# Sorting the nodes of a graph network by type, so that both typed node stages run one type per batch

## The reference, cut to what matters

```python
def typed_linear(inp_, W, b):                       # W: 3 x 256 x 256
    y = jnp.einsum('ni,tio->tno', inp_, W) + b[:, None, :]
    return y[node_type, ar]

h = relu(layernorm(x));  x = x + L0(h, ...)         # k, q, v of all nodes; edges; x + h + agg @ Wo.T + bo
h = relu(layernorm(x))                              # 6250 x 256
k, q, v = typed_linear(h, Wk, bk), typed_linear(h, Wq, bq), typed_linear(h, Wv, bv)
# per edge: softmax of q[dst] . (k[src] @ rel_att[type]) over the edges of one (dst, relation)
t_rel = segment_sum(w * (v[src] @ rel_msg[type]))   # n x 6 x 256
t = (t_rel * present).sum(1) / max(present.sum(-1), 1)
trans = typed_linear(t, Wa, ba)
alpha = sigmoid(skip)[node_type]
out = trans * alpha + h * (1 - alpha)
normed = layernorm(out) * ln_g[node_type] + ln_b[node_type]
return x + where(has_msg, normed, h)
```

## Time and profile before

| | |
|---|---|
| median of 3 runs | 4629.6 us (4625.82 to 4632.87) |
| the profiled execution | 4623.52 us, its span 4621.4 us |
| TensorE, VectorE busy | 87%, 88% of the span |
| GpSimd, ScalarE busy | 73%, 63% |
| mean granted TensorE clock | 0.929 of full |
| DMA | 945 MB, mean 205 GB/s |

### The profile page before, as it was taken

The page is one execution under the profiler, slowest core; times in us unless marked ns, Lnnn a source line. Parts: engine busy times, 40 slices in busy tenths (PEclk is TensorE's granted clock), DMA queues, the critical chain, the costliest instruction groups (busy, mean ns, idle before and its releaser), DMA issues. The chain is left out here.

```text
span 4621.4 us, 112678 instructions
## 1 busy us (share of the span) xinstructions
PE 4013.6 (87%) x23424; PEld 3321.3 (72%) x23424; DVE 4065.6 (88%) x13278; ACT 2903.7 (63%) x8405; POOL 3360.6 (73%) x3824
## 2 busy tenths in 40 slices
PE   5888888888888879999798989998988898878887
PEld 2477777777777759899577777777767776757777
DVE  6789999999999975555699999999999999978898
ACT  5755555555555533333688888888888888872222
POOL 4588888888888841010688888888888888867776
PEclk9999999999999989999888888888898888888899
DMA  4687777777777766665677777777777777766665
GB/s 157 203 252 230 227 229 227 230 228 228 229 228 229 228 156 194 203 199 185 182 207 205 205 205 205 206 205 205 205 205 205 205 205 205 205 163 196 182 183 140
DMA packets 647340, 945.24 MB, mean 205 GB/s; under 512 B 215284, under 2 KB 490461, under 8 KB 646987
## 3 DMA queue, kind: packets, MB, share of 16 engines
q0 software_dynamic: 153792, 510.82, 39.7%
q1 hardware_dynamic: 493451, 433.34, 32.3%
HBM read 772.80 MB, written 171.02 MB: 204 GB/s over the span
## 5 line engine op out<-in xcount | busy, mean ns | idle before, releaser
L1438 POOL DMA_INDIRECT kv1c<-kv_table,rec x936 | 916.5, 979 | 299.0 <-issue 175.3
L794 POOL DMA_INDIRECT kv<-kv_table,rec x864 | 920.4, 1065 | 246.8 <-issue 231.3
L1492 ACT ACTIVATE wv<-kv1c,wv 128x64 f32<-128x64 f32 x3744 | 927.7, 334 | 2.2
L1570 DVE CUSTOM_DVE_ANT_0 masked_scores<-score_p,mask 126x384 f32<-126x384 f32 x1248 | 679.8, 545 | 6.7 <-issue 3.7
L1668 PE MATMUL sum_p<-wv,hot 128*126 128x260 f32 x1872 | 615.3, 475 | 0.9 <-ACT wv L1492 0.9
L961 PE MATMUL sum_p<-msg,hot 128*126 128x256 f32 x1728 | 432.8, 394 | 190.4 <-DVE msg L917 190.4
L1630 PE MATMUL qe_p<-qrel,hotT 126*128 126x256 f32 x1872 | 547.2, 436 | 20.4 <-ACT hotT L1470 14.0
L1427 POOL TENSOR_SCALAR hot<-iota,local 128x126 f32<-128x126 f32 x936 | 549.1, 599 | 0.2 <-issue 0.2
L961 PEld LDWEIGHTS sum_p<-msg,hot 128*126 128x126 f32 x1728 | 309.0, 189 | 278.2 <-DVE msg L917 211.2
L1630 PEld LDWEIGHTS qe_p<-qrel,hotT 126*128 126x128 f32 x1872 | 427.7, 229 | 106.8 <-ACT hotT L1470 14.2
L1668 PEld LDWEIGHTS sum_p<-wv,hot 128*126 128x126 f32 x1872 | 391.5, 224 | 85.6 <-ACT wv L1492 1.7
(11 more groups left out here) (247 smaller groups left out, 10238.6 us busy)
## 6 DMA issues: line engine op xcount, KB each, us to landing
key<-segment_keys SPq DMA_DIRECT2D x312, 189.0 KB
q_blk<-q_table SPq DMA_DIRECT2D x216, 192.5 KB, 3.5
acc_table<-acc SPq DMA_DIRECT2D x312, 128.0 KB
qrel<-q_by_relation SPq DMA_DIRECT2D x312, 126.0 KB
acc_in<-acc_table SPq DMA_DIRECT2D x50, 767.8 KB
q_by_relation<-qrel SPq DMA_DIRECT2D x50, 756.0 KB
feat<-in_edge_feat_t SPq DMA_DIRECT2D x216, 128.0 KB, 3.6
agg_table<-total SPq DMA_DIRECT2D x216, 126.0 KB
```

The lines of the kernel that those rows point to most:

```text
L794: pool.indirect_dma_start(kv[k][:, t, :], None, c["kv0_d"], bass.IndirectOffsetOnAxis(ap=rec[k][:, t, 0:1].bitcast(I32), axis=0)).then_inc ...
L1438: pool.indirect_dma_start(kv[k][:, t, :], None, c["kv1_d"], bass.IndirectOffsetOnAxis(ap=rec[k][:, t, 0:1].bitcast(I32), axis=0)).then_inc ...
L1492: ins = act.activation(wv[k][:, t, h, 0:DK], kv[s][:, t, D + h * DK:D + (h + 1) * DK], ACT.Copy, scale=wv[k][:, t, h, DK:DK + 1])
L1570: dve.tensor_tensor_reduce(junk[k][:, h, :], score_p[:, h, :], mask[it.slot(4)][:], 1.0, -BIG, ALU.add, ALU.max, top[s][:, h:h + 1]).then_ ...
```

## The change

`prepare` sorts the nodes by type on the chip. From the types (126 x 50) it makes, by masks, a scan and two small products, the place of each node in a list in which each type fills whole batches of P = 128; 52 batches hold all (`BATCHES`). It writes the list as `who_d` (per place: the node's number, once clipped for reading and once beyond the table for an empty place, so that a store skips it), made by 50 products of a one-hot matrix of batches (126 x 52) with one of lanes (126 x 128), and `type_of`, the type of each batch, in SBUF.

`nodes_1` and `nodes_out` go over 52 batches in place of 50 groups. An engine that needs the type loads it into a register (`reg_load`, the row TENSOR_LOAD below) and addresses the resident weights, biases and gains by it. The masks, the masked copies, the sums over three types and the gathers of typed rows are gone. In their place GpSimd gathers the aggregate and `xh` (one table now), scatters k, v and q by relation to the rows of their nodes, gathers the accumulators (1560 numbers a node in one row) and scatters the output. `x1` and `h1` stay in the order of the list in one table.

```diff
@@ prepare
+                pe.wait_ge(in_batch_ready, 2)
+                for j in range(GROUPS):
+                    if j % LANE_STEP == 0:
+                        pe.wait_ge(in_lane_ready, j // LANE_STEP + 1)
+                    ins = pe.matmul(who_p[:], in_batch[:, j, :], in_lane[:, j, :], start=j == 0, stop=j == GROUPS - 1)
+                dve.wait_ge(kinds_loaded, 64)
+                for t in range(TYPES):
+                    link(dve.tensor_scalar(of_type[:, t, :], kind_in[:], float(t), None, ALU.is_equal))
...
+                dve.tensor_tensor(in_batch[:], lanes(lane[0:GROUP, 0:BATCHES], GROUPS), spread(batch_f[:], BATCHES),
+                                  ALU.is_equal).then_inc(in_batch_ready, 1)
+                dve.tensor_tensor(in_batch[:], in_batch[:], spread(node_id[:], BATCHES), ALU.mult).then_inc(in_batch_ready, 1)
+                for j in range(0, GROUPS, LANE_STEP):
+                    some = slice(j, j + LANE_STEP)
+                    dve.tensor_tensor(in_lane[:, some], lanes(lane[0:GROUP, :], LANE_STEP), spread(lane_f[:, some], P),
+                                      ALU.is_equal).then_inc(in_lane_ready, 1)
@@ nodes_1, GpSimd
-                    pool.indirect_dma_start(bias[k][:], None, w0["b_kvq1"],
-                                            bass.IndirectOffsetOnAxis(ap=kind_col[k][:], axis=0)
+                    pool.indirect_dma_start(agg_xh[k][:], None, c["agg_xh_d"][0:NP, :],
+                                            bass.IndirectOffsetOnAxis(ap=who_in[k][:, 0:1], axis=0)
+                    pool.indirect_dma_start(c["kv1_d"], bass.IndirectOffsetOnAxis(ap=who_out[k][:, 1:2], axis=0),
+                                            kv[k][:], None, bounds_check=NP - 1, oob_is_err=False
+                    pool.indirect_dma_start(qrel_rows, bass.IndirectOffsetOnAxis(ap=who_out[it.slot(UN)][:, 1:2], axis=0),
+                                            qrel[k][:], None, bounds_check=NP - 1, oob_is_err=False
-                run_stages(pool, GROUPS, ((1, gather),), UN)
+                run_stages(pool, BATCHES, ((0, gather), (6, scatter_kv), (7, scatter_rel)), UN)
@@ nodes_1, VectorE
-                    dve.tensor_tensor(hT_rest[k][:], hT[k][:], hT_lead[k][:], ALU.subtract).then_inc(hT_split, 1)
+                    dve.tensor_tensor(hT_rest[k][:], hT_p[:], hT_lead[k][:], ALU.subtract).then_inc(hT_split, 1)
-                run_stages(dve, GROUPS, ((6, q_rest), (2, residual), (1, kinds), (3, scale), (4, split_kinds),
-                                         (4, h_rest), (5, kvq_out), (7, rel_out)), UN)
+                run_stages(dve, BATCHES, ((6, q_rest), (2, residual), (3, scale), (4, h_rest), (5, kvq_out),
+                                          (7, rel_out)), UN)
@@ nodes_1, TensorE
+                    pe.reg_load(kind, c["type_of"][0:1, ds(it.index, 1)])
+                    t = pe.snap(kind, min_val=0, max_val=TYPES - 1)
-                        for a in range(KINDS):
+                        for a in range(HALF):
+                            row = ds(t * HALF + a, 1)
-                            pe.matmul(dst, lead, w_lead[:, a, cols], start=a == 0, stop=False)
+                            pe.matmul(dst, lead, w_lead[:, row, cols], start=a == 0, stop=False)
@@ nodes_out
-    UN = 8
+    UN = 4
-                run_stages(pool, GROUPS, ((5, affine), (0, gather), (0, means), (2, less_h)), UN)
+                run_stages(pool, BATCHES, ((0, gather), (6, gamma), (6, finish), (6, scatter)), UN)
-                run_stages(act, GROUPS, ((1, turn_out), (4, norm), (3, root)), UN)
+                run_stages(act, BATCHES, ((2, mean_out), (5, norm), (3, sum_out), (4, root)), UN)
-                run_stages(dve, GROUPS, ((3, split_kinds), (0, inverses), (4, scale), (0, kinds), (4, shifts), (0, means),
-                                         (1, turn_out), (3, transform), (1, counts), (3, mix), (1, per_relation),
-                                         (3, stats), (6, finish), (3, variance)), UN)
+                run_stages(dve, BATCHES, ((1, masses), (4, mix), (1, inverses), (5, scale), (1, means), (4, stats),
+                                          (5, scale_here), (2, at_least_one), (4, variance), (5, shifts),
+                                          (2, per_relation), (3, stays)), UN)
-                    for a in range(TYPES * HALF):
+                    for a in range(HALF):
-                run_stages(pe, GROUPS, ((1, turn), (3, project), (2, relate)), UN)
+                run_stages(pe, BATCHES, ((2, turn), (4, project), (3, relate)), UN)
```

761 lines of the change are left out of this document (425 added, 336 removed).

## The result

The changed kernel takes **4417.8 us** (median of 4, 4411.7 to 4426.1), the kernel before, measured beside it, 4627.7 us (4621.9 to 4632.9). The ratio is 0.9548, 95% interval 0.9524 to 0.9571: 210 us faster, where 121 us were forecast.

A forecast was written before the change was run, and what follows sets the result against it. TensorE was taken to bound `nodes_1` and VectorE `nodes_out`; +19 us in `prepare`, -116 in `nodes_1` and -24 in `nodes_out` made -121 against 4623.5 us, 4502.5, forecast as 4505 us. The range was 4425 to 4600 us.

The forecast's parts named there:

- the first chain: `prepare`: about 27 short dependent VectorE operations and one TensorE trip ahead of the old chain, 8 us with the loads.
- The fixed parts of `nodes_1`: `nodes_1`: 44 us outside the batches, plus 4 for a list and a gather ahead of the first batch.
- the prediction's other sign: Whole kernel: the prediction is wrong if a period misses by over 1 us or an edge stage moves over 10 us.
- rival three: `nodes_1`, `nodes_out`: idle gaps slow TensorE's clock to 0.66, about 9.6 and 9.9 us a batch, 4732 us; chance 0.07.
- rival two: `nodes_1`: transfers replace TensorE as the bound, 9 us a batch, stage 516 us, kernel 4599 us; chance 0.12.
- VectorE's chain in `nodes_1`: `nodes_1`: VectorE's operations and waits, 7.9 us before, become the bound at 7.1 us, taken as 7.2 a batch.
- that is all its slack: `nodes_1`: VectorE's only slack is its 2.0 us wait for relation products; the other 7.9 us form a chain.
- The load: `nodes_1`, `nodes_out`: a register load on TensorE or VectorE costs 0 to 1.4 us, taken as 1.0 from SyncE's gap.
- thirteen short ones at 0.18 us: `nodes_out`: thirteen short VectorE operations a batch, priced by their duration in `prepare`, 2.3 us.
- The 10 us added for a new start: `nodes_out`: 10 us more at the start, since VectorE scales the weights before the first gather may go.
- The 21 us beside the groups before: `nodes_out`: 21 us stood outside the 50 groups in the kernel before and were kept in the new stage time.
- Rival one: `nodes_1`, `nodes_out`: register loads cost nothing, 6.1 and 7.0 us a batch, 4396 us; chance 0.13.

The follow-up runs named there:

- set E: Changed kernel, and the same with both VectorE register loads earlier and `prepare`'s ranges turned earlier, measured on one chip: 4411.2 and 4373.8 us.
- out_vector_finish: Changed kernel with `nodes_out`'s load early and GpSimd's multiplication by gamma and last addition moved to VectorE: ratio 0.9531, `nodes_out` 380.5 us.

## Why the prediction was wrong, by its own steps

**What held.** The direction, the place and the order of the gains; `prepare` (+17.6 for +19: +8.1 for the 8 of the first chain, then 21.5 us from the records to the turned ranges instead of 12, +9.5 for the 11). TensorE's work in `nodes_1`, 5.7 us. The fixed parts of `nodes_1` (44 us beside 52 batches, 48 forecast). The edge stages moved by 4.5 and 3.4 us, under the 10 that would have spoken against the reading. By the prediction's other sign, a period that misses by over 1 us, `nodes_out` speaks against it: 6.60 us for 8.0. The clock was 1.00 in the steady parts of `nodes_1` and `nodes_out` (1780 to 2040 and 4100 to 4350 us) although TensorE was busy only 92% and 79% of them, so rival three did not come. Nor did rival two: TensorE waits for nothing but `q`, at 237 GB/s in the steady part.

**VectorE's chain in `nodes_1`.** That VectorE's chain becomes the bound was right: in the changed kernel it has no slack left (0.3 us of waiting for the relation products in 260). Its length was not. Per batch, in the prediction's terms:

| term | forecast | measured |
|---|---|---|
| chain before, 9.89 - 2.0 | 7.9 | 7.9 |
| masks, masked copies, narrower `hT_rest` | -2.1 | -2.0 |
| wait for ScalarE's leading part of `h1` | +0.3 | +0.11 |
| register load | +1.0 | +0.89 |
| wait for TensorE ahead of `q` | 0 | -0.25 |
| wait for ScalarE's leading part of q | 0 | -0.19 |
| hand-over, rounding | +0.1 | -0.06 |
| sum | 7.2 | 6.4 |

The step that failed is "that is all its slack, because its operations and the waits between them form a chain". The chain of 7.9 us held two more waits that could shrink, 0.25 us for TensorE's `q_p` and 0.69 us for ScalarE's leading part of q (9.9 and 27.7 us in 40 groups), and 0.44 us of them went: after the change nothing and 0.50 us are left. That is the largest part of the 0.8 us by which the batch was misjudged; the wait for ScalarE that grew by 0.11 us and not by 0.3, the load, and the hand-over make the rest. 0.8 us times 52 batches is 42 us, the stage's miss.

**The load.** On TensorE it was put at 1.0 us and shows no cost; the sum did not feel that, because VectorE's chain was taken as the longer. On VectorE it stands with 0.89 us in `nodes_1`, near its price, and with 0.56 in `nodes_out`. What it is worth is less: without it, or with it early, a batch of `nodes_1` gets shorter by 0.45 us on the chip of set E (6.37 to 5.92 us) and by 0.02 to 0.23 on three others. There VectorE waits for TensorE instead; why so much more than in set E stays open. The price came from SyncE's gap, which held a dozen register operations and a load of two numbers, while the line of the chunk counts had a load of one number on both engines at 0.31 to 0.55 us. The Trainium skill (DMA: Bandwidth & Descriptors, Latency and other measured facts) gives about 600 ns as the floor of a tensor load. This trace does not agree: its shortest is 297 ns, and the medians are 304 ns on TensorE's queue and 307 ns on VectorE's in `nodes_out`. As a price, 0.6 us would have been nearer than 1.0 in `nodes_out` and on TensorE, and farther off for VectorE in `nodes_1`.

**VectorE's sum in `nodes_out`.** Per batch, forecast and measured:

| term | forecast | measured |
|---|---|---|
| division of 1536 numbers | 1.85 | 1.76 |
| five operations of 256 numbers, with contention | 2.75 | 3.29 |
| short operations | 2.3 | 0.76 |
| load | 1.0 | 0.56 |
| other idle time, rounding | 0.1 | 0.2 |
| sum | 8.0 | 6.6 |

(VectorE is busy 220.0 of 250 us, 5.81 us a batch of 6.60; the short ones are what is left of it after the first two rows.) The failed step is "thirteen short ones at 0.18 us". 0.18 us is how long one lasts in `prepare`, where each depends on the one before and they start 0.21 us apart (39.29, 39.50 and 39.71 us). In `nodes_out` independent ones stand between long ones and follow each other every 0.06 to 0.1 us, and the kernel before showed that in its own `nodes_out`. It is 1.5 us a batch, 80 us, more than the stage's whole miss; the load, 0.56 us for 1.0, adds 23 us. Two terms stood against them: contention was taken as 0.5 us and is 0.95 (`base` and `under`), and the start and end of the stage take 46 us, not 31. The 10 us added for a new start were about right (VectorE first scales the weights, and the first gather goes out 14.3 us after the stage's start). The 21 us beside the groups before were not: they rest on 9.0 us a group in a window, while the first ten groups take 7.5 us each and all fifty 8.68 (`spread` starts at 4163.5, 4238.9 and 4588.6 us for the first, the eleventh and the last), which leaves 38 us beside them.

**Rival one** gave 6.1 and 7.0 us a batch and 4396 us, nearer than the forecast, for a reason that is half true: the load shows no cost on TensorE, and on VectorE it does. That its total is near is luck: 6.40 us lies above its 6.1 and 6.60 below its 7.0. Its "against", that VectorE waits just ahead of the load for ScalarE, was right about VectorE's queue and was no reason for TensorE's. The range ended above this rival because it had only 0.13. The bounds of the terms themselves reached to 6.4 us in `nodes_out`, but with the load hidden and no contention at once; the price of the short operations had no bound of its own, and that was the one that failed.

## What to carry to other kernels

Price a small operation by the distance to its neighbour in a place of the same kind (independent between long ones, or dependent), not by its duration. Ask the trace for the line of an operation that the change adds, even where it occurs only twice. A register load costs least behind a long operation or ahead of a wait that is there anyway: moving two of them was worth 36 us on one chip and, by the two stages, 16 to 23 us on three others. Waits inside a chain are no fixed part of it: ask of each what it waits for, and whether the change makes that quicker. And a wait removed is worth only the way to the next one: 0.89 us gave 0.45 at best, and VectorE's 0.45 us of freed time in `nodes_out` gave nothing.

## What the runs showed of the hardware

- A register load lasts 0.30 us on TensorE's and VectorE's queues in most places, but 0.73 us (median) in the changed kernel's `nodes_1`, where it stands right behind `hT_rest` in VectorE's stream; moved ahead of the wait for ScalarE its median is 0.31. Why is open.
- Short operations of VectorE on one column last 0.14 to 0.16 us each and, where none waits for the last, start every 0.06 to 0.07 us (three neighbours at 4203.49, 4203.56 and 4203.62 us). Six more of them in a batch cost at most 1.7 us in 52 batches.
- GpSimd's operation of 256 numbers (0.73 us) and VectorE's of the same size with two SBUF inputs hold each other up: VectorE's takes 0.93 to 1.07 us instead of 0.48, and GpSimd's first one in the changed kernel 0.97. With GpSimd's two operations moved to VectorE all three of VectorE's take 0.48 to 0.49 us (out_vector_finish). The Trainium skill (SBUF — State Buffer, Who interferes with whom) says that an instruction of VectorE with two SBUF inputs contends with one of GpSimd that reads SBUF, over ports that one of them locks; the trace agrees. `mass_o`, a `tensor_scalar` with one SBUF input, was held up too, 0.73 us instead of 0.17. That section has an instruction with one SBUF input free of this contention only outside the modes that use both ports, and lists `tensor_scalar` among those that can enter them; no run here shows whether `mass_o` did.
- GpSimd's indirect DMA is held up by VectorE's division, which has two SBUF inputs, when it starts while the division runs: the scatter takes 2.52 us instead of 1.03, and in the batch shown above it ends 0.9 us after the division. One that starts 0.25 us ahead of the division takes 1.04 us (the changed kernel, 4302.71 us).
